# Last stage: the scores and value products of two steps issued together, the transposes of each step behind its first projection

## The chip, the core and the metric

The kernel runs on one core of a Trainium2 chip: TensorE (PE; its weight loads are PEld), VectorE (DVE), ScalarE (ACT), GpSimd (POOL), and SyncE (SP), which issues the DMAs. Everything is in 32-bit floats. The metric is the device time of one execution in microseconds (us); lower is better.

## What is computed

A small decoder of two layers over an input of 4 x 512 tokens x 256 channels: self-attention, cross-attention and a mixture of experts, then attention, cross-attention and a local-attention network of six layers, each part followed by a layer norm. The change touches only the last part, in which 16 heads of 64 channels attend to a window of two blocks of 64 tokens:

```python
for i in range(DEPTH):                      # DEPTH = 6
    x = attn_layer(shift_tokens(x), Wqkv[i], q_scale[i], k_scale[i], Wo[i]) + x
    x = ffn_layer(shift_tokens(x), ln_g[i], ln_b[i], W1[i], b1[i], W2[i], b2[i]) + x

def attn_layer(x, Wqkv, qs, ksc, Wo):       # x @ Wqkv, split into q, k, v and 16 heads
    q = l2norm(q) * qs; k = l2norm(k) * ksc # then rotary factors on both
    out = local_attention(q, k, v)          # softmax(8 q k', mask: own block and the one before) v
    return out @ Wo
def ffn_layer(x, g, bln, W1, b1, W2, b2):   # layer norm, then a * gelu(gate), then W2
```

## The kernel before

The last stage (`stage_l1_ffn`, L169) handles 6 layers x 4 sequences = 24 bodies. A body is one layer of one sequence of 512 tokens, four tiles of 128. The order of all work in a body is written out by hand in the generator `body()` (L275); each engine walks the same list and does its own share of each entry, so the position of an entry in the list is its position in the queue of every engine. There is no scheduler: an engine never passes a waiting instruction, except that weight loads may be pulled ahead of matmuls.

A body has N = 16 steps: step n = 4 t + g treats four heads (group g) of tile t. The entries, by their names in the code:

- `s` n: scores. PE writes them into banks 4 and 5 of PSUM with 64 x 64 tiles of the array (L525). DVE adds the mask, takes the maximum and copies them to `prob` (L761), then scales the maximum into `nb` (L769). `e` n: the exponential on ACT (L655), at the end of the step, after `nb`.
- `r` m: DVE turns the sums into reciprocals (L778) and scales the probabilities (L784). It is done one step after the scores and waits for `e` m.
- `pt` m: PE transposes the probabilities of step m = n - 2 (L474, out of `prob`). The copy from PSUM to `pT` is ACT's for an even m (L621) and DVE's for an odd m (L691).
- `pv` m: the value products of step m = n - 3 at the end of the step (L554). They need the `pT` copy of m. After an odd m ACT copies the result to `oT` (L669).
- `qkv`: six projections per tile, two tiles ahead (L494, 128 x 512 each); ACT evacuates them (L639 to L641). `rot`: the rotary work and the sums of squares on DVE (L719, L721, L726), with one addition on POOL (L890). `pow` and `norm`: the norms of q and k (L732 and L742 on DVE, L895 on POOL). `tr`: transposes of q and k (L474, out of `raw`), evacuated by ACT (L648).
- Spread over the steps: the output projection `wo` (L575), the transposes `xt` of the next body's input (L474, out of `x_all`), `ln`, `xn` and `xnt` (layer norm and its transposes out of `xn`), and the network `f1g`, `f1a`, `f1p`, `f1b`, `f2` (L591, L597, L608, L614).

All transposes (`xt`, `xnt`, `tr`, `pt`) take banks 2 and 3 of PSUM in turn, in the order of the list (L325). A transpose into a bank waits until whoever evacuates the bank's earlier contents is done (`transposes`, L472). The projections and the network take banks 0, 1 and 6 in turn; `pv` takes bank 7.

The steps g = 0 to 3 differ in what follows `s`, `pt`, `r`: the list at L298 to L309 holds that, and the table below it the extra work of single steps.

## Time and profile before

| | us |
|---|---|
| median of 3 runs | 4310.21 (4306.44 to 4314.18) |
| the profiled execution, its own time | 4308.47 |
| its span (first to last instruction) | 4306.6 |
| the last stage, 24 bodies: first `s` to the end | 1328 to 4307 |
| one body in the steady part | 122.1 |

Over the whole program TensorE was busy 94% of the span, VectorE 68%, ScalarE 60%, GpSimd 29%. The time of the profiled execution is 1.9 us more than the span of its instructions. Busy times are sums over the span: an engine that is busy 68% of it can be idle where another waits, and the other way round. Matmuls overlap, so the time that a group of matmuls takes is read from its start to the start of the next group, not from its busy time. The mean granted clock of TensorE was 0.977 of full speed (2.4 GHz is the upper of its two levels).

### The profile page before, as it was taken

What the parts mean: (1) busy time and instruction counts of PE and PEld (TensorE: products, weight loads), DVE (VectorE), ACT (ScalarE), POOL (GpSimd) and SP (SyncE); (2) the same over time, 40 slices, a digit from 0 to 9 for tenths busy, and PEclk for the clock granted to TensorE, in tenths of its full rate; (3) what the DMA queues carried; (4) which work ended last, traced back from release to release, by engine and by line L of the source; (5) the groups of instructions that cost most, each with busy time, mean ns of one, the idle gap of its engine ahead of it and who ended that gap; (6) DMA issues with size and microseconds to landing.
All of it is one profiled execution on the core that took longest, in us unless ns stands there. A gap on an engine that the chain in (4) does not pass through costs nothing.

```text
span 4306.6 us, 86504 instructions
## 1 busy us (share of the span) xinstructions
PE 4033.8 (94%) x30808; PEld 2601.9 (60%) x30808; DVE 2927.6 (68%) x10261; ACT 2593.4 (60%) x6872; POOL 1239.1 (29%) x809
## 2 busy tenths in 40 slices
PE   8969388899988999999999999999999999999996
PEld 5559355666654666666666666666666666666564
DVE  3542357777776877777777777777777776777773
ACT  2214156666665766666666766666666666666652
POOL 1012300000004433333434333333334333334330
PEclk9979699999999999999999999999999999999998
DMA  5002210000002101110011101011011101111010
GB/s 185 22 29 73 62 50 2 6 17 23 9 2 63 25 16 51 28 32 23 22 45 31 36 21 45 24 37 28 16 51 31 36 21 28 40 39 28 16 36 18
DMA packets 94307, 146.62 MB, mean 34 GB/s; under 512 B 17908, under 2 KB 59744, under 8 KB 93504
## 3 DMA queue, kind: packets, MB, share of 16 engines
q1 hardware_dynamic: 90480, 131.80, 10.7%
q0 software_dynamic: 3408, 9.31, 0.8%
q8 instruction: 254, 4.16, 0.4%
q14 instruction: 165, 1.35, 0.1%
HBM read 79.36 MB, written 11.40 MB: 21 GB/s over the span
## 4 chain that ended last, share of the span: by engine, by line
PE 61%; DVE 3%; ACT 3%; issue 1%; POOL 1%; DMA 1%; SPq 0%; POOLq 0%; DVEq 0%
PE psum L494 20%; PE psum L591 9%; PE psum L474 9%; PE psum L575 7%; PE psum L554 5%; PE psum L525 5%; PE psum L608 5%; ACT f_prob L655 1%; PE psum L597 1%; POOL f_rn L895 1%; PE psum L614 1%; DVE f_rot L719 1%; DVE f_rot L721 0%; DVE f_ss L726 0%; ACT f_sq L639 0%
## 5 line engine op out<-in xcount | busy, mean ns | idle before, releaser
L494 PE MATMUL psum<-f_wqkv,f_xsT 128*128 128x512 f32 x2304 | 1076.5, 595 | 3.7 <-ACT f_raw L641 2.0
L890 POOL TENSOR_TENSOR f_raw<-f_rot 128x512 f32<-128x512 f32 x384 | 488.5, 1272 | 1748.1 <-DVE f_rot L721 1748.1
L655 ACT ACTIVATE f_prob<-f_prob,f_nb,f_rq 128x128 f32<-128x128 f32 x1536 | 740.3, 488 | 28.3 <-DVE f_nb L769 27.4
L761 DVE CUSTOM_DVE_ANT_0 f_prob<-psum,f_band 128x128 f32<-128x128 f32 x1536 | 353.7, 285 | 420.2 <-PE psum L525 418.3
L494 PEld LDWEIGHTS psum<-f_wqkv,f_xsT 128*128 128x128 f32 x2304 | 400.7, 191 | 321.5 <-issue 317.3
L895 POOL TENSOR_TENSOR f_rn<-f_ss,f_half_pow 128x32 f32<-128x32 f32 x96 | 522.6, 5444 | 11.1
L591 PE MATMUL psum<-f_xnT,f_w 128*128 128x512 f32 x960 | 438.3, 596 | 1.9 <-ACT f_xnT L676 1.1
L621 ACT COPY f_pT<-psum 128x512 f32<-128x512 f32 x192 | 111.6, 581 | 476.6 <-PE psum L474 476.6
L639 ACT ACTIVATE f_sq<-psum 128x512 f32<-128x512 f32 x384 | 229.5, 598 | 259.4 <-PE psum L494 259.3
L784 DVE TENSOR_SCALAR f_prob<-f_prob,f_rs 128x128 f32<-128x128 f32 x1536 | 350.0, 291 | 13.7 <-DVE f_rs L778 0.2
L575 PE MATMUL psum<-f_wo,f_oT 128*128 128x256 f32 x1536 | 350.9, 381 | 5.8 <-ACT f_oT L669 2.2
L719 DVE TENSOR_TENSOR f_rot<-f_raw,f_tab 128x512 f32<-128x512 f32 x384 | 333.2, 868 | 15.4 <-DMA x_before_mlp<-x_all 15.4
L575 PEld LDWEIGHTS psum<-f_wo,f_oT 128*128 128x128 f32 x1536 | 287.5, 190 | 84.8 <-ACT f_oT L669 33.8
L2046 ACT ACTIVATE h_prob<-h_prob,h_nb 128x512 f32<-128x512 f32 (+3 forms) x512 | 324.7, 639 | 0.0
L591 PEld LDWEIGHTS psum<-f_xnT,f_w 128*128 128x128 f32 x960 | 179.7, 192 | 209.6 <-issue 207.7
L655 ACT ACTIVATION_READ_ACCUMULATOR f_prob<-f_prob,f_nb,f_rq 128x1 f32 x1536 | 296.2, 193 | 0.0
L525 PE MATMUL psum<-f_kT,f_qT 64*64 64x128 f32 x6144 | 257.2, 283 | 9.3 <-DVE f_mx L761 9.3
L554 PEld LDWEIGHTS psum<-f_pT,f_v_near 128*64 128x64 f32 x3072 | 154.1, 136 | 183.5 <-issue 182.5
L1961 PEld LDWEIGHTS psum<-ident,h_prob 128*128 128x128 f32 x1664 | 184.7, 141 | 130.3 <-issue 66.2
L721 DVE TENSOR_TENSOR f_rot<-f_raw,f_tab 128x512 f32<-128x512 f32 x384 | 262.5, 683 | 0.0
L726 DVE TENSOR_REDUCE f_ss<-f_sq 128x8 f32<-128x512 f32 x384 | 259.9, 677 | 0.0
L2014 ACT COPY h_pT<-psum 128x512 f32<-128x512 f32 (+3 forms) x256 | 129.5, 506 | 214.9 <-PE psum L1961 214.9
(249 smaller groups left out, 7283.0 us busy)
## 6 DMA issues: line engine op xcount, KB each, us to landing
...
```

Source lines behind the costliest of these rows:

```text
L474: mm = nc.tensor.transpose(ps.ap(key)[:, slot * P:(slot + 1) * P], src, ident[:])
L494: mm = nc.tensor.matmul(ps.ap(step), xsT[:, c, t * P:(t + 1) * P], wqkv[:, c, i * HALF:(i + 1) * HALF], start=c == 0, stop=c == KC - 1)
L525: mm = nc.tensor.matmul(ps.ap(key)[asks, n * P:(n + 1) * P], qT[rows, 2 * g + n, asks], key_blocks(kT[rows, 2 * g + n, :], t, half), start ...
L554: mm = nc.tensor.matmul(out[n * DH:(n + 1) * DH, pair % 4 * P + half * W:pair % 4 * P + (half + 1) * W], (v if half else v_near)[:, t, h * ...
L575: mm = nc.tensor.matmul(ps.ap(step)[:, 0:D], oT[:, c, :], wo[:, c, :], start=c == 0, stop=c == OC - 1)
L591: mm = nc.tensor.matmul(ps.ap(step), w1[:, c, at:at + P], xnT[:, c, :], start=c == 0, stop=c == KC - 1)
L655: ex = nc.scalar.activation(pr, pr, ACT.Exp, bias=nb[:, t % 2, h:h + 1], scale=rq8[:, t, h:h + 1], accum_out=sums[:, t % 2, h:h + 1])
L719: nc.vector.tensor_tensor(heads(rot[:, n % 2, 0, :]), heads(q), cos, ALU.mult)
L761: red = nc.vector.tensor_tensor_reduce(prob[:, (4 * n + 2 * j + i) % 16, :], ps.ap(key)[:, j * P:(j + 1) * P], band[:, min(t, 1), :], 1.0, ...
L784: ins = nc.vector.tensor_scalar(pr, pr, rs[:, t % 2, h:h + 1], None, ALU.mult)
L890: nc.gpsimd.tensor_tensor(raw[:, (4 * t + i) % 8, :], rot[:, n % 2, 0, :], rot[:, n % 2, 1, :], ALU.add).then_inc(rope_done, 1)
L895: nc.gpsimd.tensor_tensor(rn[:, t % 2, :], ss[:, t % 2, :], half_pow[:], ALU.pow).then_inc(rn_ready, 1)
```

## The change

The list keeps its entries and changes their order, in three ways. The scores of steps n and n + 1 are issued by PE together, at the even step; banks 4 and 5 then hold four blocks of 128 columns instead of two, and DVE frees them after the odd step's share. The value products of two steps, n - 3 and n - 2, are issued together at the end of the odd step n. The transposes `pt` of the probabilities stand behind the first projection of the step (at g = 0 and g = 2 also ahead of the `tr` that stood there before). A semaphore, `even_max`, orders DVE's own maximum before its scaling in even steps. The number of matmuls and of their columns does not change.

```diff
--- before.py
+++ after.py
@@ -240,6 +240,7 @@
         ssm_ready = sem("ssm_ready")
         rn_ready = sem("rn_ready")
         qk_ready = sem("qk_ready")
+        even_max = sem("even_max")
         nb_ready = sem("nb_ready")
         exp_ready = sem("exp_ready")
         rs_ready = sem("rs_ready")
@@ -293,20 +294,20 @@
                 if n == N - 1:
                     yield ("f1b", -1)
                 yield ("s", 0, n)
-                yield ("pt", of(n - 2), n - 2)
                 yield ("r", of(n - 1), n - 1)
+                late = ("pt", of(n - 2), n - 2)
                 if g == 0:
-                    yield from [("tr", 0, t, 1, n), project(0), ("tr", 0, t, 3, n), project(4)]
+                    yield from [project(0), late, ("tr", 0, t, 1, n), project(4), ("tr", 0, t, 3, n)]
                 elif g == 1:
-                    yield from [("norm", nxt[1], nxt[0]), rotate(0), project(2)]
+                    yield from [("norm", nxt[1], nxt[0]), rotate(0), project(2), late]
                     if n == 9:
                         yield ("xnt", -1, 0)
                     yield project(1)
                 elif g == 2:
-                    yield from [("tr", nxt[1], nxt[0], 0, n), rotate(2), rotate(1), project(3),
+                    yield from [rotate(2), rotate(1), project(3), late, ("tr", nxt[1], nxt[0], 0, n),
                                 ("tr", nxt[1], nxt[0], 2, n)]
                 else:
-                    yield from [rotate(3), ("pow", ahead[1], ahead[0]), project(5)]
+                    yield from [rotate(3), ("pow", ahead[1], ahead[0]), project(5), late]
                 yield from {
                     1: [("f2", -2, 0), ("f2", -2, 1)], 3: [("wo", -1, 3)],
                     4: [("tab", 1, 0)], 5: [("f2", -2, 2), ("f2", -2, 3)], 6: [("sum", -2)],
@@ -316,7 +317,8 @@
                     14: [("f1g", -1, 4), ("f1p", -1)],
                     15: [("f1a", -1, 4), ("wo", 0, 2)]}.get(n, ())
                 yield ("e", 0, n)
-                yield ("pv", of(n - 3), n - 3)
+                if n % 2:
+                    yield from [("pv", of(n - 3), n - 3), ("pv", of(n - 2), n - 2)]
 
         full = list(body())
         banks, ring = {}, {"p": 0, "t": 0}
@@ -325,7 +327,7 @@
             if kind in ("xt", "xnt", "tr", "pt"):
                 banks[step] = 2 + ring["t"] % 2
                 ring["t"] += 1
-            elif kind == "s":
+            elif kind == "s" and step[2] % 2 == 0:
                 for i in range(2):
                     banks[step + (i,)] = 4 + i
             elif kind == "pv" and step[2] % 2 == 0:
@@ -502,7 +504,7 @@
                         else:
                             pe.wait_ge(qk_ready, (it + off) * 2 * TB + 2 * t + i - 1)
                         transposes(step, it, [(n, raw[:, (4 * t + i) % 8, n * P:(n + 1) * P]) for n in range(4)])
-                    elif kind == "s":
+                    elif kind == "s" and step[2] % 2 == 0:
                         t, g = divmod(step[2], G)
                         if g == 0:
                             for i in (0, 2):
@@ -516,18 +518,20 @@
                         for i in range(2):
                             key = step + (i,)
                             pe.wait_ge(ps.sem_drained(key), ps.before(key, it))
-                        for n in range(2):
-                            for half in range(2):
-                                for i in range(2):
-                                    key = step + (i,)
-                                    rows = slice(i * DH, (i + 1) * DH)
-                                    asks = slice(half * W, (half + 1) * W)
-                                    mm = nc.tensor.matmul(ps.ap(key)[asks, n * P:(n + 1) * P],
-                                                          qT[rows, 2 * g + n, asks],
-                                                          key_blocks(kT[rows, 2 * g + n, :], t, half),
-                                                          start=True, stop=True)
-                                    if n == half == 1:
-                                        mm.then_inc(ps.sem_filled(key), 1)
+                        for m in (0, 1):
+                            for n in range(2):
+                                for half in range(2):
+                                    for i in range(2):
+                                        key = step + (i,)
+                                        rows = slice(i * DH, (i + 1) * DH)
+                                        asks = slice(half * W, (half + 1) * W)
+                                        at = (2 * m + n) * P
+                                        mm = nc.tensor.matmul(ps.ap(key)[asks, at:at + P],
+                                                              qT[rows, 2 * (g + m) + n, asks],
+                                                              key_blocks(kT[rows, 2 * (g + m) + n, :], t, half),
+                                                              start=True, stop=True)
+                                        if m == n == half == 1:
+                                            mm.then_inc(ps.sem_filled(key), 1)
                     elif kind == "pt":
                         m = step[2]
                         pe.wait_ge(prob_ready, it * N + m + 1)
@@ -539,12 +543,8 @@
                             pe.wait_ge(ps.sem_drained(out_key(m)), ps.before(out_key(m), it))
                         if g == 0:
                             pe.wait_ge(near_ready[t], (it + off + 1) * (32 if t else 16))
-                        if m >= -2:
-                            wait_drained(pe, ps, ("pt", off, m), it)
-                            out = ps.ap(out_key(m))
-                        else:
-                            wait_drained_in_last_body(pe, ps, ("pt", 0, m + N), it)
-                            out = ps.previous.ap(out_key(m + N))
+                        wait_drained(pe, ps, ("pt", off, m), it)
+                        out = ps.ap(out_key(m))
                         for i in range(2):
                             pair = 2 * g + i
                             for half in range(2):
@@ -661,10 +661,7 @@
                     elif kind == "pv" and step[2] % 2 == 1:
                         m = step[2]
                         g = m % G
-                        if m >= -2:
-                            out, n = ps.ap(out_key(m)), ps.count(out_key(m), it)
-                        else:
-                            out, n = ps.previous.ap(out_key(m + N)), ps.in_last_body(out_key(m + N), it)
+                        out, n = ps.ap(out_key(m)), ps.count(out_key(m), it)
                         act.wait_ge(shared["filled"][7], n)
                         nc.scalar.copy(oT[:, 4 * (g // 2):4 * (g // 2) + 4, :],
                                        out.rearrange("p (n q) -> p n q", q=P)).then_inc(shared["drained"][7], 1)
@@ -753,19 +750,25 @@
                             seen = ps.in_last_body(old, it)
                             if seen is not None:
                                 dve.wait_ge(shared["filled"][ps.previous.bank[old]], seen)
+                        both = ("s", 0, n - n % 2)
                         for i in range(2):
-                            key = step + (i,)
+                            key = both + (i,)
                             wait_filled(dve, ps, key, it)
                             for j in range(2):
                                 h = 4 * g + 2 * j + i
                                 red = nc.vector.tensor_tensor_reduce(
                                     prob[:, (4 * n + 2 * j + i) % 16, :],
-                                    ps.ap(key)[:, j * P:(j + 1) * P],
+                                    ps.ap(key)[:, (n % 2 * 2 + j) * P:(n % 2 * 2 + j + 1) * P],
                                     band[:, min(t, 1), :], 1.0, LOWEST, ALU.add, ALU.max,
                                     mx[:, t % 2, h:h + 1])
-                            red.then_inc(ps.sem_drained(key), 1)
-                        for i in range(2):
-                            wait_drained(dve, ps, step + (i,), it)
+                            if n % 2:
+                                red.then_inc(ps.sem_drained(key), 1)
+                        if n % 2:
+                            for i in range(2):
+                                wait_drained(dve, ps, both + (i,), it)
+                        else:
+                            red.then_inc(even_max, 1)
+                            dve.wait_ge(even_max, it * (N // 2) + n // 2 + 1)
                         nc.vector.scalar_tensor_tensor(
                             out=nb[:, t % 2, 4 * g:4 * g + 4], in0=mx[:, t % 2, 4 * g:4 * g + 4], scalar=-1.0,
                             in1=rq8[:, t, 4 * g:4 * g + 4], op0=ALU.mult, op1=ALU.mult).then_inc(nb_ready, 1)
```

TensorE's order in steps 6 and 7 of a steady body, before (`f_prob` is `pt`, `f_raw` is `tr`, `x_all` is `xt`; the bank that an instruction waits for stands behind it):

```order
L525 MATMUL psum<-f_kT,f_qT 64x128 [waits bank4_drained,bank5_drained,bank2_drained,bank3_drained]
L474 MATMUL psum<-ident,f_prob 128x128 [waits bank2_drained,f_prob_ready]
L474 MATMUL psum<-ident,f_raw 128x128 [waits bank3_drained,f_rope_done]
L494 MATMUL psum<-f_wqkv,f_xsT 128x512 [waits bank0_drained]
L474 MATMUL psum<-ident,f_raw 128x128 [waits bank2_drained,f_qk_ready]
L554 MATMUL psum<-f_pT,f_v_near 64x64 [waits bank3_drained]
L525 MATMUL psum<-f_kT,f_qT 64x128 [waits bank5_drained,bank4_drained]
L474 MATMUL psum<-ident,f_prob 128x128 [waits bank3_drained,f_prob_ready]
L494 MATMUL psum<-f_wqkv,f_xsT 128x512 [waits bank1_drained]
L474 MATMUL psum<-ident,x_all 128x128 [waits bank2_drained,f_x_ready]
L575 MATMUL psum<-f_wo,f_oT 128x256 [waits bank7_drained,bank6_drained,f_wo_landed]
L474 MATMUL psum<-ident,x_all 128x128 [waits bank3_drained,f_x_ready]
```

And of the change:

```order
L529 MATMUL psum<-f_kT,f_qT 64x128 [waits bank4_drained,bank5_drained,bank2_drained,bank3_drained]
L496 MATMUL psum<-f_wqkv,f_xsT 128x512 [waits bank0_drained]
L476 MATMUL psum<-ident,f_prob 128x128 [waits bank2_drained,f_prob_ready]
L476 MATMUL psum<-ident,f_raw 128x128 [waits bank3_drained,f_rope_done]
L476 MATMUL psum<-ident,f_raw 128x128 [waits bank2_drained,f_qk_ready]
L496 MATMUL psum<-f_wqkv,f_xsT 128x512 [waits bank1_drained]
L476 MATMUL psum<-ident,f_prob 128x128 [waits bank3_drained,f_prob_ready]
L476 MATMUL psum<-ident,x_all 128x128 [waits bank2_drained,f_x_ready]
L575 MATMUL psum<-f_wo,f_oT 128x256 [waits bank7_drained,bank6_drained,f_wo_landed]
L476 MATMUL psum<-ident,x_all 128x128 [waits bank3_drained,f_x_ready]
L554 MATMUL psum<-f_pT,f_v_near 64x64 [waits bank2_drained,f_near_ready1,bank7_drained]
L554 MATMUL psum<-f_pT,f_v_near 64x64 [waits bank3_drained]
```

The list of before ends ahead of the value products of step 4, which stand alone there. The second half of the scores has gone from step 7 to step 6. In step 6 the three transposes (`pt`, `tr`, `tr`) now follow one another, and the third goes to the bank of the first. In step 7 the `pt` of an odd step, which DVE evacuates, is followed by `xt` and, after `wo`, by a second `xt` into the same bank 3.

VectorE's order in step 7, before, from the scaled maximum (L769) to the addition of `wo` (L789):

```order
L769 SCALAR_TENSOR_TENSOR f_nb<-f_mx,f_rq 128x4 [waits bank5_drained,bank4_drained]
L691 COPY f_pT<-psum 128x512 [waits bank3_filled]
L778 RECIPROCAL f_rs<-f_sums 128x4 [waits f_exp_ready]
L784 TENSOR_SCALAR f_prob<-f_prob,f_rs 128x128 [waits f_rs_ready]
L784 TENSOR_SCALAR f_prob<-f_prob,f_rs 128x128 x3
L719 TENSOR_TENSOR f_rot<-f_raw,f_tab 128x512 [waits f_rope_done,bank0_drained]
L721 TENSOR_TENSOR f_rot<-f_raw,f_tab 128x512
L726 TENSOR_REDUCE f_ss<-f_sq 128x8 [waits f_sq_ready]
L732 TENSOR_SCALAR f_ss<-f_ss 128x32 [waits f_ss_ready]
L789 TENSOR_TENSOR x_all<-psum,x_all 128x256 [waits bank6_filled]
```

And of the change (L772 is the scaled maximum, L688 the copy, L792 the addition):

```order
L772 SCALAR_TENSOR_TENSOR f_nb<-f_mx,f_rq 128x4 [waits bank5_drained,bank4_drained]
L781 RECIPROCAL f_rs<-f_sums 128x4 [waits f_exp_ready]
L787 TENSOR_SCALAR f_prob<-f_prob,f_rs 128x128 [waits f_rs_ready]
L787 TENSOR_SCALAR f_prob<-f_prob,f_rs 128x128 x3
L716 TENSOR_TENSOR f_rot<-f_raw,f_tab 128x512 [waits f_rope_done,bank0_drained]
L718 TENSOR_TENSOR f_rot<-f_raw,f_tab 128x512
L723 TENSOR_REDUCE f_ss<-f_sq 128x8 [waits f_sq_ready]
L729 TENSOR_SCALAR f_ss<-f_ss 128x32 [waits f_ss_ready]
L688 COPY f_pT<-psum 128x512 [waits bank3_filled]
L792 TENSOR_TENSOR x_all<-psum,x_all 128x256 [waits bank6_filled]
```

The copy to `pT` has moved behind the scaling of the probabilities (L787), the rotary work (L716 to L723) and the `pow` step (L729). Everything else keeps its place.

TensorE's order in step 9, of the change, up to the first value products of the pair (`f_xn` is `xnt`):

```order
L496 MATMUL psum<-f_wqkv,f_xsT 128x512 [waits bank6_drained,f_qkv_landed2]
L476 MATMUL psum<-ident,f_prob 128x128 [waits bank3_drained,f_prob_ready]
L476 MATMUL psum<-ident,f_xn 128x128 [waits bank2_drained,f_xn_ready]
L496 MATMUL psum<-f_wqkv,f_xsT 128x512 [waits bank0_drained,f_qkv_landed1]
L476 MATMUL psum<-ident,f_xn 128x128 [waits bank3_drained,f_xn_ready]
L554 MATMUL psum<-f_pT,f_v_near 64x64 [waits bank2_drained,bank7_drained]
```

Before, `pt` stood ahead of the first of the two projections and the value products of step 6 behind it all; here `pt` of step 7 and the second `xnt` share bank 3, and DVE's copy of that `pt` stands behind `norm` (L734, L739) and `rot` in its queue.

## Rows read from the trace of the kernel before

**Rows 1.** Stretch: us, busy PE, PEld, DVE, ACT, POOL (instructions), clock, DMA, GB/s.

```profile
2500.00:3000.00 500.00, 499.54 (x3715) 310.06 (x3716) 367.17 (x1364) 339.92 (x882) 188.37 (x118) 1.00 0.12 31
```

**Rows 2.** TensorE's timeline, scores of a body's even steps: start, busy us, line, operation, count.

```profile
2516.41 0.67 PE L525 MATMUL psum<-f_kT,f_qT 64*64 64x128 f32 x16
...
2532.71 0.56 PE L525 MATMUL psum<-f_kT,f_qT 64*64 64x128 f32 x12
...
2544.43 0.67 PE L525 MATMUL psum<-f_kT,f_qT 64*64 64x128 f32 x16
...
2560.72 0.67 PE L525 MATMUL psum<-f_kT,f_qT 64*64 64x128 f32 x16
...
2573.03 0.67 PE L525 MATMUL psum<-f_kT,f_qT 64*64 64x128 f32 x16
...
2585.42 0.67 PE L525 MATMUL psum<-f_kT,f_qT 64*64 64x128 f32 x16
...
2603.76 0.67 PE L525 MATMUL psum<-f_kT,f_qT 64*64 64x128 f32 x16
...
2621.97 0.67 PE L525 MATMUL psum<-f_kT,f_qT 64*64 64x128 f32 x16
...
2638.49 0.67 PE L525 MATMUL psum<-f_kT,f_qT 64*64 64x128 f32 x16
```

**Rows 3.** TensorE's timeline in steps 6 and 7.

```profile
2561.32 0.66 PE L474 MATMUL psum<-ident,f_prob 128*128 128x128 f32 x4
2561.81 0.60 PE L474 MATMUL psum<-ident,f_raw 128*128 128x128 f32 x4
2562.25 1.88 PE L494 MATMUL psum<-f_wqkv,f_xsT 128*128 128x512 f32 x4
2563.97 0.60 PE L474 MATMUL psum<-ident,f_raw 128*128 128x128 f32 x4
2564.50 0.34 PE L554 MATMUL psum<-f_pT,f_v_near 128*64 128x64 f32 x4
2564.66 0.29 PE L554 MATMUL psum<-f_pT,f_v 128*64 128x64 f32 x4
...
2564.90 0.29 PE L554 MATMUL psum<-f_pT,f_v 128*64 128x64 f32 x4
2565.11 0.67 PE L525 MATMUL psum<-f_kT,f_qT 64*64 64x128 f32 x16
...
2568.36 3.68 PE L575 MATMUL psum<-f_wo,f_oT 128*128 128x256 f32 x16
```

**Rows 4.** TensorE's timeline, first body: projections right behind scores that began at 1336.14.

```profile
1336.74 3.70 PE L494 MATMUL psum<-f_wqkv,f_xsT 128*128 128x512 f32 x8
```

**Rows 5.** VectorE's timeline in steps 6 and 7: scores, reciprocals of step 7, addition.

```profile
2561.55 0.29 DVE L761 CUSTOM_DVE_ANT_0 f_prob<-psum,f_band 128x128 f32<-128x128 f32 x1 [0.58 <-PE psum L525]
...
2569.67 0.17 DVE L778 RECIPROCAL f_rs<-f_sums 128x4 f32<-128x4 f32 x1
...
2573.26 0.41 DVE L789 TENSOR_TENSOR x_all<-psum,x_all 128x256 f32<-128x256 f32 x1
```

**Rows 6.** ScalarE's timeline in steps 8 and 9: first exponential, and behind a projection.

```profile
2579.11 0.49 ACT L655 ACTIVATE f_prob<-f_prob,f_nb,f_rq 128x128 f32<-128x128 f32 x1
...
2582.15 0.60 ACT L639 ACTIVATE f_sq<-psum 128x512 f32<-128x512 f32 x1 [0.55 <-PE psum L494]
```

**Rows 7.** VectorE's timeline: reciprocals in step 15 (of the body before) and in step 13.

```profile
2511.26 0.18 DVE L778 RECIPROCAL f_rs<-f_sums 128x4 f32<-128x4 f32 x1 [0.52 <-ACT f_prob L655]
...
2616.85 0.18 DVE L778 RECIPROCAL f_rs<-f_sums 128x4 f32<-128x4 f32 x1 [0.91 <-ACT f_prob L655]
...
2620.93 1.40 DVE L819 SCALAR_TENSOR_TENSOR f_hT<-psum,f_b1a,f_hT 128x512 f32<-128x512 f32 x2
```

**Rows 8.** Stretches in a cross-attention, before and behind the end of a gap.

```profile
174.40:177.80 3.40, 1.40 (x5) 0.55 (x5) 1.02 (x5) 1.77 (x4) 0.00 (x0) 0.99 0.03 11
177.80:181.20 3.40, 3.40 (x6) 1.34 (x5) 0.75 (x1) 0.00 (x0) 0.00 (x0) 0.50 0.02 5
```

## The prediction

> **What bounds the kernel now.** I read the shares of the page first: TensorE leads by far. Then the busy times by stretch. In the steady part of the last stage TensorE is busy 499.54 of 500 us at full clock, while VectorE has 367 and ScalarE 340 [rows 1]. So TensorE's queue sets the time there and the other engines have room, on average. The timeline of TensorE shows how regular it is: a body takes 2638.49 - 2516.41 = 122.08 us, and its eight pairs of steps take 16.30, 11.72, 16.29, 12.31, 12.39, 18.34, 18.21 and 16.52 us [rows 2]. An average hides what a pair of 12 us means, so I read VectorE's timeline beside it: in steps 6 and 7 VectorE works from 2561.55 to the addition at 2573.26 with no idle time, 11.71 us in a pair of 12.31 [rows 5, 2]. In short pairs it is as full as TensorE; it costs nothing now because its copy of `pT` stands early in its queue and is used a step later.
>
> **What the change saves.** The price of changing from one kind of matmul to the next is in the starts [rows 3]. Transposes to value products: 0.53 us from start to start instead of 0.44, so 0.09. The first four value matmuls take 0.16 instead of 0.12 (0.04), the last four 0.21 (0.09). Sixteen score matmuls take 0.60 us to the next kind; four more of them cost 0.11 (busy 0.67 for sixteen, 0.56 for twelve [rows 2]), so 0.16 of the 0.60 is entry and exit. The `pt` behind them takes 0.49 instead of 0.44, so 0.05. Sum 0.43, read to two digits; I take 0.45. A pair pays this twice, 0.90. Afterwards it pays one round without the 0.05, plus what a projection pays behind scores: eight take 3.70 us busy where four take 1.88 [rows 4, 3], 1.82 for the other four instead of 1.72, so 0.10. The pair pays 0.50 and saves 0.40: 3.2 us a body, 77 us in 24 bodies. That the projection goes ahead of `pt` thus saves nothing by itself. Bounds: 0 if the price is not one of the kind (a rival below), 0.45 if the projection hides its 0.10.
>
> The tiling page of the Trainium skill (TensorEngine Tiling (Array Packing), Key Properties) says that a change of the tiling mode drains TensorE, and TensorE: Matmul & The Clock Gate (Single matmul latency) gives about 175 ns for the drain. Three changes fewer a pair would then be, as an estimate, 3 x 0.175 x 8 x 24 = 101 us. The rows give 77, and the sum goes by them.
>
> **What it adds: the copy comes last, the value products come early.** `pv` of an odd step m = n - 2 now ends step n, in whose middle its `pt` stands, and VectorE's copy stands behind rotary work in its queue. I walk each kind of pair from the start of its joint scores, 0. These take 0.60 + 4 x 0.11 = 1.04 us. Today VectorE starts 0.83 us after the scores' start (2561.55 - 2560.72 [rows 5, 2]); the bank is now released by the last group of 32, 0.44 later: 1.27.
>
> Pair (2,3) and pair (6,7). VectorE's chain from scores to addition keeps its contents, with the copy last: 1.27 + 11.71 = 12.98, and the copy's modelled end is 0.08 later; TensorE follows at 13.1 (I allow 0.05 for the signal). TensorE itself needs 1.04, projection 1.82, `pt` 0.44, `tr` 0.44, a wait (next paragraph), `tr` 0.44, projection 1.72, `pt` 0.44, `wo` 3.5 [rows 3], first products 0.6: it is there at 11.4 and waits 1.7 us. The second products (0.61) end the pair at 13.72, against 11.72: +2.00. In pair (6,7) it is worse, since the second `xt` goes to the bank of the `pt` of step 7 and must wait for the same copy: TensorE is there at 11.2, starts at 13.1, and only then follow `xt` 0.49, the change 0.09 and both products 0.61 + 0.47: 14.78, against 12.31: +2.47.
>
> The wait in every step g = 2: `pt`, `tr`, `tr` now follow one another, and the third takes the bank of the first. The projection ends at 2.86. ScalarE starts some 0.2 us after a projection, and its square, its copy and the copy of `pt` (0.5 to 0.6 us each [rows 6]) end at about 4.6. TensorE would be there at 3.74. So 0.9 us, between 0 (ScalarE ahead of this) and 1.2; taken as 0.9. It is hidden in pairs (2,3) and (6,7), where VectorE is later, and shows in (10,11) and (14,15).
>
> Pair (8,9). Today the first exponential of step 8 starts at 2579.11, 6.08 after the scores [rows 6, 2], 0.67 behind TensorE's last evacuated work (0.60 + 0.49 + 2 x 0.44 + 2 x 1.72 = 5.41). That work now ends at 5.90, so the exponentials start at 6.57 and, four of 0.49 and the hand-over, release VectorE at 8.62. Reciprocals, scaling, `norm` and `rot` take 4.08 (2620.93 - 2616.85 [rows 7]); the copy runs from 12.70 to 13.38, and TensorE's second `xnt`, in the bank of that `pt`, starts at 13.43, though TensorE was there at 10.2. Then 0.49 + 0.09 + 1.08: 15.09 against 12.39, +2.70.
>
> Pair (12,13): the reciprocals start 13.09 after the scores today [rows 7, 2]; TensorE's part ahead of them is 5.90 instead of 5.41, so 13.58; + 4.08 + 0.68 + 0.05 = 18.39, + 0.61 = 19.00 against 18.21: +0.79. Pair (14,15): the reciprocals start at 2511.26, 11.37 after their scores (the body before this one), waiting for ScalarE; TensorE's part ahead is 8.53 instead of 7.13, so 12.77; to the copy 3.59 (2573.26 - 2569.67 [rows 5]), copy 0.73, products 0.61: 17.70 against 16.52, +1.18.
>
> Pairs (0,1) and (4,5): VectorE's copy would be done by about 13.4, TensorE comes at 15.3 behind `f2`. Covered, -0.40 each; that cover is worth 1.9 us. Pair (10,11): copy at about 16.9, TensorE at 18; -0.40 + 0.9 = +0.51 with the rounding.
>
> Sum of a body: -0.80 + 2.00 + 2.47 + 2.70 + 0.51 + 0.79 + 1.18 = +8.85 us; 24 bodies: +212. The first two bodies lack the network's work, so that their pairs fall to the limits of 13.7 to 15 us too; the last has no rotary work in its second half: +5 together, an estimate. Sum +217.
>
> **The clock.** In a cross-attention TensorE stood idle for 2.0 of 3.4 us, and in the next 3.4 us its clock was 0.50, the lower level [rows 8]. The new gap in pair (8,9) is 3.2 us long, those of (2,3) and (6,7) 1.7 to 1.9. A stretch of 3.4 us at half speed costs 1.7 us, and pair (10,11) has no slack for it. I take one in 20 of 24 bodies, +34; the bounds are 0 and two in each body, +82.
>
> TensorE: Matmul & The Clock Gate of the Trainium skill (Why this matters for your kernels) asks for no idle gaps over about 3 us. By that only the gap in pair (8,9) counts. Rows 8 show a fall behind a shorter one, and the trace decides; the sum is the same, and the 1.9 us gaps are in the upper bound.
>
> So 4308.5 (the profiled execution) + 217 + 34 = 4560; that execution is 1.7 us under the median of the runs, so 4562.
>
> **Rivals.** (a) The waits come as worked out, but the clock stays up: 4310 + 217 = 4527. For it: the gap ends inside dense work; against: rows 8. (b) The cover holds, and the change does only what it removes: 4310 - 77 = 4233, the case on the faster side. It decides at the copy in step 7: it needs VectorE's chain of 11.71 us to be under 9.8, by an overlap that the timeline does not show, or a copy that is not in the order of the queue. For it: VectorE has 27% idle time; against: none of it in steps 2, 3, 6 and 7. (c) Only the bank waits of steps 7 and 9 are real and the others are covered: 2.47 + 2.70 less six times 0.40 = +2.8 a body, 4377. (d) The change does not do what it says: the price of a change of kind comes back elsewhere, in the three pairs that TensorE sets and partly in (8,9) to (14,15), 1.7 us a body: 4603.
>
> **Chances.** The forecast 0.53, with 4530 to 4600 for itself; (a) 0.29; (d) 0.06; (c) 0.05; (b) 0.05; within 0.2% of before (9 us, what a measurement can tell from nothing) 0.02. Slower 0.93, same 0.02, faster 0.05. The range 4460 to 4615 takes in (a) with its lower bound of the waits (0.9 at g = 2 gone, 1 us less in pair (8,9)), and leaves out (b), (c) and the far end of the clock.
>
> **What would show it.** TensorE busy 92 to 94% of a stretch of 500 us instead of 99.9; a body of 131 to 133 us; joint scores of 1.04 us; waits of TensorE for the copy of `pT` (L688) of 1.7 us in step 3, 1.9 ahead of the second `xt`, 3.2 ahead of the second `xnt`, 0.9 for ScalarE's `pT` copy ahead of the second `tr` of g = 2. A clock of 0.50 for some 3.4 us in pair (10,11) of most bodies speaks for the forecast against (a). A body under 122 us would make it wrong, and so would waits at places other than these.

## The result, and the profile after

| | before | after |
|---|---|---|
| median, us | 4311.74 (4306.44 to 4314.18, 4 runs) | 4568.2 (4567.48 to 4577.24, 4 runs) |
| ratio | 1 | 1.0601 (95%: 1.0583 to 1.062) |
| TensorE busy, share of the span | 94% | 88% |
| mean granted clock | 0.977 | 0.969 |

The change makes the kernel 6% slower; 4562 was predicted. From the profile's page of the kernel after: the engines' shares, and the chain of work that ended last, by engine:

```profile
PE 4019.1 (88%) x30808; PEld 2640.9 (58%) x30808; DVE 2919.3 (64%) x10261; ACT 2603.5 (57%) x6872; POOL 1239.1 (27%) x809
...
PE 41%; DVE 19%; ACT 7%; issue 3%; DMA 1%; POOL 0%; SPq 0%; DVEq 0%; POOLq 0%; ACTq 0%
```

No engine is full any more: TensorE waits, and a fifth of the chain runs through VectorE, where it was 3% before. The stretches of the kernel after (columns as in [rows 1]): the one that answers to [rows 1], a body whose clock stays up, and three around the end of a gap in another body:

```profile
2500.00:3000.00 500.00, 456.64 (x3488) 294.54 (x3487) 339.31 (x1268) 310.71 (x818) 179.37 (x109) 0.99 0.11 31
2638.11:2769.29 131.18, 119.87 (x912) 76.24 (x908) 88.97 (x333) 83.11 (x216) 46.46 (x30) 1.00 0.07 18
2836.28:2839.70 3.42, 3.42 (x15) 1.71 (x13) 2.00 (x12) 3.42 (x11) 0.00 (x0) 1.00 0.03 5
2839.70:2843.10 3.40, 0.17 (x2) 0.08 (x2) 3.21 (x6) 1.11 (x3) 1.26 (x1) 1.00 0.00 0
2843.10:2846.50 3.40, 3.40 (x48) 2.95 (x52) 0.00 (x0) 2.38 (x8) 0.00 (x0) 0.50 0.00 0
```

TensorE is busy 456.64 of 500 us, 91.3%, where [rows 1] have 499.54; the prediction had 92 to 94%. A body takes 131.18 us instead of 122.08. The last three lines answer to [rows 8]: TensorE works 0.17 of 3.40 us, VectorE nearly all of it, and the clock is at its lower level for the next 3.4 us.

What TensorE waits for, steady stretch 1700 to 4000 (17 to 18 bodies): total us, times, longest:

```profile
PE psum L476 <- DVE f_pT L688: 83.9, 34, 3.4
PE psum L476 <- ACT f_pT L621: 60.3, 69, 0.9
PE psum L554 <- DVE f_pT L688: 51.3, 53, 1.5
```

So each body has two transposes (steps 7 and 9) and three value products (steps 3, 13 and 15) that wait for VectorE's copy, and four transposes (each g = 2) that wait for ScalarE's. All are waits for evacuations of `pt`. In the same stretch of the kernel before TensorE has a single wait, of 0.3 us, and none of these. TensorE's timeline in steps 6 to 9 answers to [rows 3] (start, busy us, idle before it and what ended that):

```profile
2684.56 1.98 PE L496 MATMUL psum<-f_wqkv,f_xsT 128*128 128x512 f32 x4
2686.38 0.60 PE L476 MATMUL psum<-ident,f_prob 128*128 128x128 f32 x4
2686.82 0.60 PE L476 MATMUL psum<-ident,f_raw 128*128 128x128 f32 x4
2688.29 0.63 PE L476 MATMUL psum<-ident,f_raw 128*128 128x128 f32 x4 [0.87 <-ACT f_pT L621]
2688.76 1.88 PE L496 MATMUL psum<-f_wqkv,f_xsT 128*128 128x512 f32 x4
2690.47 0.60 PE L476 MATMUL psum<-ident,f_prob 128*128 128x128 f32 x4
2690.91 0.60 PE L476 MATMUL psum<-ident,x_all 128*128 128x128 f32 x4
2691.35 3.62 PE L575 MATMUL psum<-f_wo,f_oT 128*128 128x256 f32 x16
2696.65 0.63 PE L476 MATMUL psum<-ident,x_all 128*128 128x128 f32 x4 [1.69 <-DVE f_pT L688]
...
2698.29 1.10 PE L529 MATMUL psum<-f_kT,f_qT 64*64 64x128 f32 x32
...
2711.88 0.63 PE L476 MATMUL psum<-ident,f_xn 128*128 128x128 f32 x4 [3.23 <-DVE f_pT L688]
```

And VectorE in step 7, which answers to [rows 5]: from the scores' share to the copy there is no idle time. `pt` (2690.47) was done by 2691.1, and its copy starts at 2695.83.

```profile
2691.15 0.27 DVE L759 CUSTOM_DVE_ANT_0 f_prob<-psum,f_band 128x128 f32<-128x128 f32 x1
...
2692.45 0.88 DVE L787 TENSOR_SCALAR f_prob<-f_prob,f_rs 128x128 f32<-128x128 f32 x4
...
2695.16 0.75 DVE L729 TENSOR_SCALAR f_ss<-f_ss 128x32 f32<-128x32 f32 x1
2695.83 0.68 DVE L688 COPY f_pT<-psum 128x512 f32<-128x512 f32 x1
2696.43 0.41 DVE L792 TENSOR_TENSOR x_all<-psum,x_all 128x256 f32<-128x256 f32 x1
```

ScalarE's first exponential of step 8, which answers to [rows 6], and VectorE's reciprocals of steps 13 and 15 with the copies behind them, which answer to [rows 7]:

```profile
2704.90 0.51 ACT L655 ACTIVATE f_prob<-f_prob,f_nb,f_rq 128x128 f32<-128x128 f32 x1
```
```profile
2745.99 0.18 DVE L781 RECIPROCAL f_rs<-f_sums 128x4 f32<-128x4 f32 x1 [9.01 <-ACT f_prob L655]
2750.07 0.68 DVE L688 COPY f_pT<-psum 128x512 f32<-128x512 f32 x1
...
2764.35 0.18 DVE L781 RECIPROCAL f_rs<-f_sums 128x4 f32<-128x4 f32 x1 [1.14 <-ACT f_prob L655]
2767.95 0.68 DVE L688 COPY f_pT<-psum 128x512 f32<-128x512 f32 x1
```

The eight pairs of a steady body, from the starts of even steps' scores (us; median over the 20 steady bodies, the third to the 22nd; for after and late_only those of a body without a fall of the clock). "Body" is the median body, for after and late_only again one without a fall; "mean" is the mean of the 20 bodies, falls included. "Falls" counts how often in these 20 bodies the clock went to 0.50. Of the bodies of spread none is without a fall, so its pairs hold what the clock costs. The kernels of the experiments are in the same table:

| kernel | 0,1 | 2,3 | 4,5 | 6,7 | 8,9 | 10,11 | 12,13 | 14,15 | body | mean | falls |
|---|---|---|---|---|---|---|---|---|---|---|---|
| before | 16.30 | 11.72 | 16.30 | 12.31 | 12.39 | 18.34 | 18.21 | 16.52 | 122.08 | 122.11 | 0 |
| predicted | 15.90 | 13.72 | 15.89 | 14.78 | 15.09 | 18.85 | 19.00 | 17.70 | 130.93 | | |
| after | 15.88 | 13.65 | 15.88 | 14.76 | 15.23 | 18.88 | 19.02 | 17.87 | 131.18 | 132.45 | 16 |
| filled_gap | 15.88 | 13.64 | 15.88 | 14.76 | 15.15 | 18.88 | 19.00 | 17.85 | 131.06 | 131.17 | 1 |
| copy_early | 15.88 | 12.01 | 15.88 | 12.89 | 12.65 | 18.88 | 17.80 | 17.16 | 123.16 | 123.20 | 0 |
| copy_mid | 15.91 | 12.01 | 15.88 | 12.89 | 13.26 | 18.88 | 17.80 | 17.16 | 123.81 | 123.84 | 0 |
| late_only | 16.39 | 12.52 | 16.39 | 13.93 | 14.31 | 19.39 | 18.31 | 17.67 | 128.90 | 129.74 | 10 |
| spread | 15.88 | 14.08 | 16.86 | 16.05 | 16.48 | 18.01 | 19.01 | 16.74 | 133.12 | 133.14 | 53 |
| pairs_only | 15.84 | 10.90 | 15.84 | 11.78 | 13.75 | 17.78 | 17.75 | 16.06 | 119.70 | 119.73 | 0 |
| pairs_xn | 15.84 | 10.90 | 15.84 | 11.78 | 12.03 | 17.78 | 17.75 | 16.06 | 117.98 | 118.01 | 0 |
| copy_early_spread | 15.88 | 10.91 | 15.88 | 11.78 | 13.75 | 17.77 | 17.80 | 16.06 | 119.83 | 119.95 | 1 |
| value_pair | 16.15 | 11.22 | 16.15 | 12.09 | 13.08 | 18.20 | 18.06 | 16.37 | 121.32 | 121.35 | 0 |
| score_pair | 16.13 | 12.15 | 16.13 | 12.75 | 12.33 | 18.07 | 18.05 | 16.72 | 122.35 | 122.37 | 0 |

### The profile page after: what moved, and what is told of

Its sections match the earlier page's. It is cut to its first block, busy times and chain, and to the rows that moved or that the text cites. A ratio compares the mean times of both kernels' runs of the same rounds, so it can differ in the third digit from the quotient of the medians.

```text
span 4566.1 us, 86120 instructions
## 1 busy us (share of the span) xinstructions
PE 4019.1 (88%) x30808; PEld 2640.9 (58%) x30808; DVE 2919.3 (64%) x10261; ACT 2603.5 (57%) x6872; POOL 1239.1 (27%) x809
## 4 chain that ended last, share of the span: by engine, by line
PE 41%; DVE 19%; ACT 7%; issue 3%; DMA 1%; POOL 0%; SPq 0%; DVEq 0%; POOLq 0%; ACTq 0%
PE psum L496 14%; PE psum L591 6%; PE psum L529 5%; PE psum L476 4%; PE psum L608 4%; PE psum L554 4%; DVE f_rot L716 4%; ACT f_prob L655 3%; DVE f_ss L723 3%; DVE f_rot L718 3%; DVE f_prob L787 3%; PE psum L575 2%; DVE f_prob L759 2%; DVE f_pT L688 2%; DVE f_raw L739 1%
## 5 line engine op out<-in xcount | busy, mean ns | idle before, releaser
L496 PE MATMUL psum<-f_wqkv,f_xsT 128*128 128x512 f32 x2304 | 1112.1, 606 | 6.0 <-ACT f_raw L641 4.4
L781 DVE RECIPROCAL f_rs<-f_sums 128x4 f32<-128x4 f32 x384 | 66.7, 174 | 559.3 <-ACT f_prob L655 559.0
L787 DVE TENSOR_SCALAR f_prob<-f_prob,f_rs 128x128 f32<-128x128 f32 x1536 | 336.5, 283 | 13.6
L716 DVE TENSOR_TENSOR f_rot<-f_raw,f_tab 128x512 f32<-128x512 f32 x384 | 334.1, 870 | 15.1 <-DMA x_before_mlp<-x_all 15.1
L666 ACT COPY f_oT<-psum 128x512 f32<-128x512 f32 x192 | 111.9, 583 | 406.5 <-PE psum L554 406.5
L476 PE MATMUL psum<-ident,f_raw 128*128 128x128 f32 x1536 | 234.0, 275 | 87.1 <-ACT f_pT L621 82.8
L476 PEld LDWEIGHTS psum<-ident,f_prob 128*128 128x128 f32 x1536 | 192.3, 141 | 201.4 <-issue 198.3
L554 PE MATMUL psum<-f_pT,f_v_near 128*64 128x64 f32 x3072 | 218.4, 238 | 94.8 <-DVE f_pT L688 94.8
L476 PEld LDWEIGHTS psum<-ident,f_raw 128*128 128x128 f32 x1536 | 178.7, 141 | 158.3 <-issue 153.7
```

The costliest lines, as they stand in the source:

```text
L476: mm = nc.tensor.transpose(ps.ap(key)[:, slot * P:(slot + 1) * P], src, ident[:])
L496: mm = nc.tensor.matmul(ps.ap(step), xsT[:, c, t * P:(t + 1) * P], wqkv[:, c, i * HALF:(i + 1) * HALF], start=c == 0, stop=c == KC - 1)
L554: mm = nc.tensor.matmul(out[n * DH:(n + 1) * DH, pair % 4 * P + half * W:pair % 4 * P + (half + 1) * W], (v if half else v_near)[:, t, h * ...
L716: nc.vector.tensor_tensor(heads(rot[:, n % 2, 0, :]), heads(q), cos, ALU.mult)
L787: ins = nc.vector.tensor_scalar(pr, pr, rs[:, t % 2, h:h + 1], None, ALU.mult)
```

## The experiments

My theory was: the pairing saves some 0.4 us a pair; the late `pt` costs, because the DVE copy of an odd `pt` stands behind rotary work in VectorE's queue and the bank ring hands that delay to `xt` and `xnt`; and a long gap costs clock. The rival explanations: the pairing itself costs, or ScalarE's waits at g = 2 do, or the clock does.

**copy_early: DVE's copy goes back to its old place.** TensorE's order is that of the change. In VectorE's queue the copy of an odd step stands right behind the scores, ahead of the reciprocals (`r`), `norm`, `rot` and `pow`.

```diff
-                yield ("r", of(n - 1), n - 1)
                 late = ("pt", of(n - 2), n - 2)
+                if n % 2 == 0:
+                    yield ("r", of(n - 1), n - 1)
+                r = ("r", of(n - 1), n - 1)
@@ g == 1
-                    yield from [("norm", nxt[1], nxt[0]), rotate(0), project(2), late]
+                    yield from [project(2), late, r, ("norm", nxt[1], nxt[0]), rotate(0)]
@@ g == 3
-                    yield from [rotate(3), ("pow", ahead[1], ahead[0]), project(5), late]
+                    yield from [project(5), late, r, rotate(3), ("pow", ahead[1], ahead[0])]
```

> The changed kernel with TensorE's order as it is; in odd steps VectorE copies pT right behind the scores, ahead of the reciprocals, norm, rot and pow. Theory (the loss is the place of this copy in VectorE's queue): the waits for it in steps 3, 7, 9, 13 and 15 go, the 0.4 us a pair that the joined matmuls save stay, and so does the wait of the third transpose at g = 2 (0.9 us, now seen in four pairs a body): 122.5 us a body, 4320 us in all (4295 to 4345), and no stretch of clock 0.50 in the steady bodies. Rival (TensorE's new order is itself what costs, by the banks and by value products that come early): over 4450 us, with the same waits under another name.

Measured: 4329.53 us (4323.73 to 4341.71), ratio 1.0041 (1.0023 to 1.0059). 239 of the 258 us are gone, the clock's falls with them. TensorE has no wait for VectorE's copy left. What stays is a wait for `xn` at step 9, and the bank wait of g = 2, in TensorE's timeline of copy_early:

```profile
2603.65 0.66 PE L478 MATMUL psum<-ident,f_xn 128*128 128x128 f32 x4 [0.63 <-DVE f_xn L815]
...
2612.24 0.63 PE L478 MATMUL psum<-ident,f_raw 128*128 128x128 f32 x4 [0.87 <-ACT f_pT L623]
```

The second of these occurs four times a body. With it the third transpose starts 1.47 us after the second (2612.24 - 2610.77), where one follows the other in 0.44; so it costs 1.03.

**copy_mid: the copy between `r` and the rotary work.** `r` stays where the change has it; `project(2), late` (and `project(5), late`) go ahead of `norm` and `rot`.

```diff
-                    yield from [("norm", nxt[1], nxt[0]), rotate(0), project(2), late]
+                    yield from [project(2), late, ("norm", nxt[1], nxt[0]), rotate(0)]
@@ g == 3
-                    yield from [rotate(3), ("pow", ahead[1], ahead[0]), project(5), late]
+                    yield from [project(5), late, rotate(3), ("pow", ahead[1], ahead[0])]
```

> The changed kernel with VectorE's copy of pT behind the reciprocals and the scaling of the probabilities, but ahead of norm, rot and pow; TensorE's order as it is. Theory (the rotary work in front of the copy is what TensorE waits for; the exponentials, for which the reciprocals wait, are in time): as copy_early, 4330 us (4315 to 4345). Rival (the wait for the exponentials of the step before is enough to hold the copy up): steps 9, 13 and 15 keep waits of 1 us or more, 4390 us or more.

Measured: 4350.36 us (4348.01 to 4353.35), ratio 1.009 (1.0071 to 1.0109). That is over the range that I had given. Seven of eight pairs are those of copy_early to 0.03 us; only (8,9) differs, 13.26 instead of 12.65, since the copy is still 0.42 us late for the second `xnt`:

```profile
2605.12 0.66 PE L476 MATMUL psum<-ident,f_xn 128*128 128x128 f32 x4 [0.62 <-DVE f_xn L813]
...
2607.92 0.63 PE L476 MATMUL psum<-ident,f_xn 128*128 128x128 f32 x4 [0.42 <-DVE f_pT L688]
```

So the reciprocals and the scaling ahead of the copy cost next to nothing (0.65 us a body); the rotary work, `norm` and `pow` ahead of it cost the rest.

**pairs_only: the pairing alone, `pt` right behind the scores as before.**

```diff
                 yield ("s", 0, n)
+                yield ("pt", of(n - 2), n - 2)
                 yield ("r", of(n - 1), n - 1)
-                late = ("pt", of(n - 2), n - 2)        # and every `late` below; `tr` back in its places
```

> The kernel before with only the pairs: scores of two steps together, value products of two steps together, the transposes pt in their old place. Theory: the pairs save 0.46 us each (one round of changes between kinds of matmul of 0.46 us) and VectorE's copy, second in its queue behind the scores, is always in time: 118.4 us a body, 4222 us in all (4205 to 4250). Rival (value products in the same step as their transposes can't be covered): waits for the pT copy in steps 3, 7 and 9, over 4330 us. Rival (the price is not one of the kind): 4300 to 4320 us.

Measured: 4250.41 us (4248.49 to 4253.84), ratio 0.9864 (0.9843 to 0.9885). The pairing is a gain, of 0.46 to 0.56 us in six pairs and 0.82 in (2,3). In (2,3) of before the output projection starts 2.00 us after the projection ahead of it (2540.19 - 2538.19), in pairs_only 1.71 (2513.68 - 2511.97): it waited a little for ScalarE's `oT` copy, and value products that come a step sooner take that away. The time came out above my expectation of 4222 because pair (8,9) lost 1.36 against before. TensorE, VectorE and GpSimd of pairs_only:

```profile
2555.86 0.66 PE L476 MATMUL psum<-ident,f_xn 128*128 128x128 f32 x4 [1.67 <-DVE f_xn L813]
```
```profile
2553.66 0.35 DVE L813 TENSOR_SCALAR f_xn<-x_all,f_mv,f_rstd 128x128 f32<-128x128 f32 x1 [1.91 <-POOL f_rstd L908]
```
```profile
2547.21 5.44 POOL L898 TENSOR_TENSOR f_rn<-f_ss,f_half_pow 128x32 f32<-128x32 f32 x1
2552.62 1.01 POOL L908 TENSOR_TENSOR f_rstd<-f_rstd,f_half_pow 128x4 f32<-128x4 f32 x1
```

GpSimd's power of 4 columns for the layer norm waits behind one of 32 columns (5.44 us); with TensorE faster, the chain GpSimd, `xn`, `xnt` is late.

**pairs_xn: pairs_only with `xn` and both `xnt` later in step 9.**

```diff
+                if n == 9:
+                    yield ("xn", -1)                   # behind pt; before: in step 8
-                    if n == 9:
-                        yield ("xnt", -1, 0)           # from between the projections
@@ the table of extra work
+    8: [("end", -2)], 9: [("xnt", -1, 0), ("xnt", -1, 1)]
```

> The pairs alone (4250 us, where pair (8,9) takes 13.75 us instead of the 11.93 that the matmuls need), with two entries moved: xn from the end of step 8 to step 9 behind pt, so that VectorE copies pT of step 7 while it waits for GpSimd's rstd, and both xnt behind the second projection of step 9. Theory (TensorE waits there only for xn, and this wait is covered by a projection): pair (8,9) 11.9 to 12.1 us, 24 x 1.7 = 42 us, 4208 us (4195 to 4225). Rival (the wait passes on to the pT copy or to step 10, since VectorE is full there): 4240 to 4255 us.

Measured: 4212.85 us (4208.86 to 4222.7), ratio 0.9779 (0.9761 to 0.9798): the best version, 2.2% faster than before, 7.8% faster than the change. Pair (8,9) takes 12.03, and TensorE is full:

```profile
2500.00:3000.00 500.00, 500.00 (x3888) 323.72 (x3885) 378.57 (x1409) 348.55 (x913) 198.14 (x125) 1.00 0.12 33
...
2538.31 1.09 PE L476 MATMUL psum<-ident,f_xn 128*128 128x128 f32 x8
```

**late_only: the late `pt` alone**, scores and value products single as before.

```diff
-                yield ("pt", of(n - 2), n - 2)
                 yield ("r", of(n - 1), n - 1)
+                late = ("pt", of(n - 2), n - 2)        # placed as in the change
```

> The kernel before with only the transposes pt behind the first projection of their step; scores and value products stay single, value products a step behind. Theory (the late transposes bring the late copy, and the banks pass it on): no wait of value products, but the second xnt of step 9 waits some 3.4 us for the copy, the second xt of step 7 some 0.5, the third transpose of g = 2 some 0.9 four times, and 0.05 a step for projections behind scores: 8 us a body, 4500 us (4450 to 4540). Rival (the loss comes from value products being issued too early, the late copy alone is covered): 4310 to 4345 us.

Measured: 4482.14 us (4480.21 to 4492.31), ratio 1.0407 (1.0382 to 1.0431). So the place of `pt` alone costs 170 us. The waits, TensorE's timeline of late_only:

```profile
2607.68 0.63 PE L474 MATMUL psum<-ident,f_raw 128*128 128x128 f32 x4 [0.87 <-ACT f_pT L621]
...
2645.03 0.63 PE L474 MATMUL psum<-ident,x_all 128*128 128x128 f32 x4 [0.35 <-DVE f_pT L691]
...
2659.34 0.63 PE L474 MATMUL psum<-ident,f_xn 128*128 128x128 f32 x4 [1.81 <-DVE f_pT L691]
```

They are shorter than in the change (1.69 and 3.23), which has the pairing too: there TensorE comes to the same place 1.0 us sooner after the start of the pair's scores, and VectorE, which starts behind 32 score matmuls, copies 0.36 to 0.46 later. The expectation came true in part by luck: it had 3.4 us at the second `xnt`, where 1.81 came, and nothing for the clock, whose ten falls cost 0.84 us a body. With the pairing on top, the late `pt` costs 131.18 - 119.70 = 11.48 us a body at full clock, without it 128.9 - 122.08 = 6.8.

**value_pair and score_pair: each half of the pairing alone, on the kernel before.**

```diff
-                yield ("pv", of(n - 3), n - 3)
+                if n % 2:
+                    yield from [("pv", of(n - 3), n - 3), ("pv", of(n - 2), n - 2)]
```

That is value_pair; score_pair has the scores' part of the diff of the change (banks 4 and 5 with four blocks, `even_max`), and each `pv` where it was.

> The kernel before with only the value products joined, at the end of odd steps; scores single, transposes pt in their old place. Theory (a price per change of kind, 0.14 to 0.17 us each, whatever the kinds): in an even step transposes or a projection are followed by scores directly, one change instead of two; 0.15 us a pair, 28 us, 4283 us (4270 to 4300), where pair (8,9) may give back some. Rival (the price is one of the value products' own entry and exit, 0.23 us): 44 us, 4266 us.

> The kernel before with only the scores joined, at even steps; value products single. Theory (a price per change of kind): in an odd step value products are followed by the transposes directly, one change instead of two; 0.16 us a pair, 31 us, 4280 us (4265 to 4300). With value_pair it then makes less than the 0.46 us a pair of both together, since two neighbours of different kinds count as one excursion. Rival (each kind has a price of its own, they add): the two savings sum to that of both together.

Measured: value_pair 4285.29 us (4283.81 to 4292.87), ratio 0.9943 (0.9926 to 0.9961); score_pair 4311.68 us (4307.73 to 4322.13, 10 runs), 1.0006 (0.9996 to 1.0016). The first was as expected: 0.15 a pair in (0,1), (4,5) and (12,13), 0.50 in (2,3) by the sooner `oT` copy, and again 0.69 given back at (8,9). The second wasn't: where TensorE sets the time it saves 0.16 to 0.17 a pair ((0,1), (4,5), (12,13)) and 0.27 in (10,11), but three others lose 0.20 to 0.44. In step 3, and in step 7, of score_pair:

```profile
2542.49 3.69 PE L578 MATMUL psum<-f_wo,f_oT 128*128 128x256 f32 x16 [0.71 <-ACT f_oT L672]
```
```profile
2570.94 3.69 PE L578 MATMUL psum<-f_wo,f_oT 128*128 128x256 f32 x16 [0.43 <-ACT f_oT L672]
```

The output projection now waits for ScalarE's `oT` copy, which stands behind the exponentials. VectorE releases those later, since the bank of the scores is now full 0.44 us later: in (2,3) the first exponential starts 5.32 us after the scores instead of 4.88, the `oT` copy 7.24 instead of 6.81, and (2,3) and (6,7) lose 0.43 and 0.44. In pairs_only, where `pv` has moved too, the copy is made at the start of (2,3), and nothing is lost.

**spread: `pt` and the two `tr` of g = 2 apart again, in the change.** If the 0.87 us wait for ScalarE at g = 2 is what costs, this repairs it.

```diff
@@ g == 2
-                    yield from [rotate(2), rotate(1), project(3), late, ("tr", nxt[1], nxt[0], 0, n), ("tr", nxt[1], nxt[0], 2, n)]
+                    yield from [("tr", nxt[1], nxt[0], 0, n), rotate(2), rotate(1), project(3), late, ("tr", nxt[1], nxt[0], 2, n)]
```

> The changed kernel with one thing moved: at g = 2 the first tr stands ahead of the projection again, so that no third transpose follows two others. Theory: the 0.9 us wait for ScalarE's copy goes; it shows in pairs (10,11) and (14,15) alone, since VectorE's copy sets the others: 1.8 us a body, 43 us, 4525 us (4505 to 4545). Rival (VectorE sets those pairs as well): within 10 us of the changed kernel.

Measured: 4586.7 us (4581.48 to 4588.22), ratio 1.0639 (1.0616 to 1.0662): slower than the change, by 18 us, where I expected 43 less. The small wait is gone, but VectorE's copy is as late as ever, and TensorE collects the time in fewer, longer gaps. The stretch, and three waits of spread:

```profile
2500.00:3000.00 500.00, 461.05 (x3414) 300.26 (x3413) 338.80 (x1262) 310.39 (x813) 176.10 (x109) 0.96 0.11 30
```
```profile
2674.77 0.48 PE L554 MATMUL psum<-f_pT,f_v_near 128*64 128x64 f32 x4 [2.52 <-DVE f_pT L688]
...
2705.79 1.09 PE L476 MATMUL psum<-ident,x_all 128*128 128x128 f32 x4 [2.79 <-DVE f_pT L688]
...
2722.29 1.08 PE L476 MATMUL psum<-ident,f_xn 128*128 128x128 f32 x4 [3.22 <-DVE f_pT L688]
```

The clock fell 53 times in 20 bodies instead of 16, seven times for 6.8 us instead of 3.4. The table of pairs separates the two terms. The saving came where it was expected and a little larger: (10,11) takes 0.87 us less than in the change at full clock and (14,15) 1.13 less, 2.0 a body, 48 us. The other pairs, in which or ahead of which the clock falls, take 3.95 us more ((2,3), (4,5), (6,7), (8,9)); the falls of the change cost it 1.27 a body, so spread pays 2.7 more, 64 us. Together +16, where +18 was measured. That these 3.95 are all the clock's is not shown, since spread has no body without a fall.

**copy_early_spread: the lists of copy_early and of spread together.**

```diff
@@ g == 1 and g == 3 as in copy_early, g == 2:
+                    yield from [("tr", nxt[1], nxt[0], 0, n), rotate(2), rotate(1), project(3), late, ("tr", nxt[1], nxt[0], 2, n)]
```

> As copy_early (4330 us), and at g = 2 the first tr ahead of the projection again. It differs from pairs_only in the place of pt behind the first projection and of the reciprocals behind the copy. Theory (the third of three transposes costs 0.9 us at each g = 2 once VectorE's copy no longer hides it; without it the late pt is worth nothing or a little): pairs (2,3), (6,7), (10,11), (14,15) lose 0.9 to 1.1 us each, 24 x 3.8 = 91 us less at most, 4245 us (4235 to 4265), beside pairs_only with 4250. Rival (as in the changed kernel, the wait only moves): 4310 us or more.

Measured: 4259.28 us (4254.02 to 4266.81), ratio 0.9879 (0.986 to 0.9899). With the copy early, the spread order saves 1.1 us in each of the pairs (2,3), (6,7), (10,11) and (14,15), of which the wait for ScalarE is 1.03, and gives 1.1 back in (8,9), which again waits for `xn`. In one of its 20 bodies this wait was 2.05 us long, and the clock fell behind it. Beside pairs_only (4250.41) this says that a `pt` behind the projection is worth nothing by itself.

**filled_gap: the change, with TensorE kept busy in the gap of step 9.** Before the second `xnt` it issues three more matmuls of 512 columns into a bank that is free; their results are not used.

```diff
+    o = ("o", 0, 6)                                    # a projection bank
+    if c == 1 and o in ps.bank:
+        pe.wait_ge(ps.sem_drained(o), ps.before(o, it))
+        for _ in range(3):
+            nc.tensor.matmul(ps.ap(o), xsT[:, 0, 0:P], wqkv[:, 0, 0:HALF], start=True, stop=True, skip_group_check=True)
```

> The changed kernel with three projections more in step 9, ahead of the second xnt, into the bank that the next value products overwrite: 128 x 512 each, 0.86 us, 2.6 us of the 3.2 us in which TensorE waits there; their results are not used. Theory (the waits alone make a body of 131.2 us, and the 1.5 us above that in 16 of 20 steady bodies are the clock's): no stretch of 0.50 behind step 9, pair (8,9) 15.2 to 15.3 and (10,11) 18.9 in every body, 24 x 0.8 x 1.5 = 29 us less than the changed kernel, 4540 us (4530 to 4550). Rival (the clock's share is small or the fall comes from the waits of steps 3 and 7): 4560 to 4575 us.

Measured: 4534.05 us (4528.22 to 4540.5), ratio 1.0523 (1.0501 to 1.0545), 34 us less than the change, with more work. The three matmuls (each of 32-bit floats is two in the records), what is left of the wait, and a steady stretch with the clock up:

```profile
2686.87 2.74 PE L585 MATMUL psum<-f_wqkv,f_xsT 128*128 128x512 f32 x6
2690.15 0.66 PE L476 MATMUL psum<-ident,f_xn 128*128 128x128 f32 x4 [0.55 <-DVE f_pT L694]
```
```profile
2500.00:3000.00 500.00, 466.17 (x3511) 294.23 (x3508) 340.86 (x1270) 315.30 (x818) 177.68 (x113) 1.00 0.10 27
```

Pair for pair it is, to 0.08 us, the change in a body whose clock stays up. So the gap's length is VectorE's, and filling it gives back only the clock.

## Why the prediction was right

**The direction and the size of the waits.** Predicted 4562, measured 4568. Each pair of the table is within 0.2 us of its sum: the largest misses are (14,15), 17.87 for 17.70, and (8,9), 15.23 for 15.09. The terms inside hold too: the exponentials of step 8 start 2704.90 - 2698.29 = 6.61 after the scores (6.57 predicted), the reciprocals of step 13 start 2745.99 - 2732.40 = 13.59 (13.58), with the copy 4.08 behind (4.08). Those of step 15 start 2764.35 - 2751.42 = 12.93 (12.77), which is the miss of (14,15); the wait at g = 2 ahead of them costs 1.03 from start to start instead of 0.9, and that may be most of it. So the body adds 9.10 us at full clock, where +8.85 was worked out. The mechanism was isolated: with only the copy moved (copy_early) 8.02 of the 9.10 are gone, and with the bank order of g = 2 mended as well (copy_early_spread) the body is 2.25 under before. So the change is a gain of 2.4 us a body from the pairing, a loss of 3.5 from three transposes in a row with `pt` behind the projection (pairs_only to copy_early), a loss of 8.0 from the late copy, and 1.3 of clock on the mean. TensorE's share in the steady stretch, 91.3%, lies just under the 92 to 94% that were to show it.

**The single waits.** Ahead of the second `xt` 1.69 (1.9 predicted), ahead of the second `xnt` 3.23 (3.2), at g = 2 0.87 (0.9), at places named. The value products of steps 13 and 15 wait too, 1.0 and 0.5 us; the walk through the pairs has the copy set their end, but the list of what would show it leaves them out. The wait of step 3 is 1.41, not 1.7:

```profile
2667.03 0.34 PE L554 MATMUL psum<-f_pT,f_v_near 128*64 128x64 f32 x4 [1.41 <-DVE f_pT L688]
```

The pair's end was right all the same (13.65 for 13.72), since VectorE sets it: I had TensorE arrive 0.2 us too early, and VectorE done 0.1 too late. The same holds ahead of `xt`, by 0.2.

**The saving.** 0.40 a pair was predicted; (0,1) and (4,5), where nothing waits, show 0.42. The pairing with `pt` in its old place gives 0.46 there (0.45 by the prediction's terms), and late `pt` costs 0.04: it saves nothing, as predicted. The two halves alone save 0.15 and 0.16 or 0.17 in (0,1), (4,5) and (12,13), together 0.46. A count of the changes from one kind of matmul to another fits this: a pair has six before, two steps of transposes to value products to scores to transposes. Value products together leave five, scores together leave five, both leave three. One change fewer saves 0.15 to 0.17 us and three save 0.46, which is 0.15 each on the mean.

The Trainium skill's figure for the drain (TensorE: Matmul & The Clock Gate, Single matmul latency) had given, as an estimate, 0.525 a pair for the three changes. The runs show 0.46, and the measurement decides.

**The clock.** +34 was taken, for 20 falls in 24 bodies. In the 20 steady bodies 16 were seen; each starts in (8,9), 0.0 to 1.5 us after the end of the gap of step 9, and runs into (10,11), and none follows the gaps of 1.4 to 1.7 us. They cost 1.27 us a body, 1.6 each. filled_gap gives 4568.2 - 4534.05 = 34 us, but that the two figures agree is in part luck: some 26 us of it lie in the 20 steady bodies and the rest in the four at the ends, where the sum had counted 1.4 us a body. So rival (a), 4527, is refuted: it had the waits right and the clock wrong, and its time is that of filled_gap but for 7 us.

The rule of the Trainium skill (TensorE: Matmul & The Clock Gate, Why this matters for your kernels), no idle gaps over about 3 us, agrees with the change (3.23 us). It does not with spread and late_only, which have falls at waits of 2.52 and 1.81 us; there the measurement decides.

**The other rivals.** (b) needed VectorE's copy to have cover: its queue was full from 2691.15 to 2696.84, as the rows above show. (c) and (d) fall with the table: six of the eight pairs were not "covered", and (0,1) and (4,5) keep their 0.42, so the changes of kind are not paid again elsewhere.

**What was off.** The four bodies at the ends. The 20 steady ones were to lengthen by 8.85 + 1.42 = 10.27 us each, clock included, and did by 10.34 (132.45 - 122.11). The others were to lengthen by 4 x 10.27 + 5 = 46 and did by 54: the first two by 21.8 (97.52 to 119.33) and 17.9 (113.47 to 131.36), the last two by 12.9 and 1.7. These are the 8 us by which the profiled executions differ more (4568.04 - 4308.47 = 259.6) than the 251 of the sum. In the first two bodies the clock was at its lower level for 31.7 us instead of 6.8, which the +5 did not have.

Four of my expectations for the experiments missed: score_pair (the `oT` copy), pairs_only (the `xn` chain), spread (the clock) and, by 5 us, copy_mid (0.42 us at the second `xnt`). In the first two I had taken off a cost and overlooked what was late next; in spread I had taken the number of falls as given.
